# Attention scores of four heads on four 32-row groups of TensorE, strips written through device memory, and GpSimd splitting rotated queries and keys in batches 1 to 7

## What is computed

```python
xn = _layernorm(x, axis=-1)
# attention, on xn
q = (xn @ wq).reshape(B, T, H, D)
lat = xn @ w_down
k = (lat @ wk_up).reshape(B, T, H, D)
v = (lat @ wv_up).reshape(B, T, H, D)
q, k = _apply_rope(q, cos, sin), _apply_rope(k, cos, sin)
scores = einsum('bqhd,bkhd->bhqk', q, k) * scale
allowed = pages[None, :] <= pages[:, None]      # pages of 32 tokens
attn = softmax(where(allowed, scores, min))
s = einsum('bhqk,bkhd->bqhd', attn, v).reshape(B, T, E) @ wo
# experts, on xn: router of two layers, softmax over the best two
y = xn + sum over experts of w * (silu(xn @ ew1 + eb1) @ ew2 + eb2)
out = x + s * silu(y)
```

## Time and profile before

| | us |
|---|---|
| median of 3 runs | 585.58 |
| lowest and highest | 583.09, 585.88 |
| profiled execution | 584.54 |
| its span, first to last instruction | 582.7 |
| mean granted clock of TensorE | 0.938 of full speed |

### The profile page before, as it was taken

One profiled execution on the slowest core, in us unless ns is written; L12 is line 12 of the kernel. 1 busy time (PEld: TensorE's weight loads), 2 busy tenths in 40 slices (PEclk: granted clock), 3 DMA queues, 4 the chain that ended last, 5 costly groups with the idle time before them and its releaser, 6 DMA issues.

```text
span 582.7 us, 9046 instructions
## 1 busy us (share of the span) xinstructions
PE 499.0 (86%) x3223; PEld 327.8 (56%) x3223; DVE 387.7 (67%) x704; ACT 333.9 (57%) x504; POOL 136.7 (23%) x143
## 2 busy tenths in 40 slices
PE   3489997997699878999999999999999987778891
PEld 1256654554356444686776866767767554345450
DVE  4888585897577756836556675557674777568871
ACT  2065573654365435577876767767768543335870
POOL 3120000007664764000000000000001466553620
PEclk9767997999999997999999999999999987789997
DMA  6842216112222322748367263474222225523443
GB/s 176 282 96 102 74 37 165 29 29 82 79 75 61 92 74 65 212 128 238 112 166 190 50 183 100 104 197 118 72 66 59 67 63 161 144 64 101 117 114 90
DMA packets 64676, 64.60 MB, mean 111 GB/s; under 512 B 11096, under 2 KB 48088, under 8 KB 64120
## 3 DMA queue, kind: packets, MB, share of 16 engines
q1 hardware_dynamic: 53616, 47.89, 30.3%
q0 software_dynamic: 4096, 8.40, 5.3%
q10 hardware_dynamic: 6920, 7.74, 4.3%
HBM read 32.27 MB, written 21.24 MB: 92 GB/s over the span
## 4 chain that ended last, share of the span: by engine, by line
PE 65%; DVE 12%; ACT 7%; issue 5%; another core or an unknown queue 4%; DMA 4%; SPq 2%; POOL 1%; ACTq 0%; DVEq 0%; POOLq 0%
PE ring L610 13%; PE wide L650 10%; PE ring L630 9%; PE ring L705 6%; DVE row_max L946 6%; PE ring L695 5%; PE ring L569 4%; ACT probs L807 3%; PE ring L633 3%; PE ring L618 2%; PE ring L662 2%; PE ring L634 2%; PE ring L686 2%; PE ring L560 1%
## 5 line engine op out<-in xcount | busy, mean ns | idle before, releaser
L807 ACT ACTIVATE probs<-ring 128x768 f32<-128x768 f32 (+1 forms) x192 | 164.6, 880 | 147.1 <-PE ring L634 65.9
L946 DVE TENSOR_REDUCE row_max<-ring 128x4 f32<-128x512 f32 (+2 forms) x192 | 195.4, 1042 | 79.3 <-PE ring L610 46.2
L610 PE MATMUL ring<-k_head,q_stack 108*128 108x256 f32 (+2 forms) x512 | 132.8, 373 | 27.1 <-issue 10.9
L1142 POOL DMA_INDIRECT pair_in<-y_rows,place x64 | 62.5, 976 | 265.8 <-PE wide L650 245.2
L610 PEld LDWEIGHTS ring<-k_head,q_stack 108*128 108x128 f32 x512 | 80.6, 203 | 63.6 <-issue 30.1
L1129 POOL DMA_INDIRECT slot_rows<-xn,place x64 | 62.8, 981 | 133.5 <-PE wide L650 109.2
L650 PE MATMUL wide<-probs,v_cols 128*32 128x512 f32 (+3 forms) x1024 | 93.2, 461 | 0.8 <-ACT probs L807 0.8
L630 PE MATMUL ring<-q_stack,k_head 128*128 128x512 f32 (+1 forms) x256 | 82.7, 422 | 13.0 <-ACT probs L807 5.3
L630 PEld LDWEIGHTS ring<-q_stack,k_head 128*128 128x128 f32 x256 | 43.7, 203 | 34.2 <-issue 16.0
L650 PEld LDWEIGHTS wide<-probs,v_cols 128*32 128x32 f32 x1024 | 24.2, 111 | 36.4 <-issue 27.6
L798 ACT ACTIVATE k_head<-k_stack,hmask 128x512 fp32r<-128x512 f32 x64 | 40.8, 712 | 6.5 <-DMA k_stack<-roped_lo 5.4
(11 more groups left out here) (123 smaller groups left out, 500.1 us busy)
## 6 DMA issues: line engine op xcount, KB each, us to landing
area<-w_pack SPq DMA_DIRECT2D x39, 321.0 KB, 3.1
area<-slot_rows SPq DMA_DIRECT2D x39, 128.0 KB, 3.4
y_rows<-work SPq DMA_DIRECT2D x39, 128.0 KB, 2.7
slot_rows<-pair_in ACTq DMA_DIRECT2D x4, 1024.0 KB, 6.0
k_stack<-roped_hi SPq DMA_DIRECT2D x64, 64.0 KB
q_stack<-roped_hi SPq DMA_DIRECT2D x64, 64.0 KB
k_stack<-roped_lo SPq DMA_DIRECT2D x32, 64.0 KB
q_stack<-roped_lo SPq DMA_DIRECT2D x32, 64.0 KB
```

The lines of the kernel that those rows point to most:

```text
L610: last = mm(ps[:, at // T, at % T:at % T + width], q_stack[0:MAX0, g, i * P:(i + 1) * P], k_head[0:MAX0, GH * g + r, 0:width], start=True, ...
L807: activation(probs[:, n % 2, 2 * half:2 * half + 2, lo:T], ps[:, :, lo:T], ACT.Exp, scale=SCALE).then_inc(exp_done, 1)
L946: reduce(row_max[:, g, i, heads[0]:heads[-1] + 1], ps[:, :, 0:(i + 1) * P], AX, ALU.max).then_inc(max_done, 1)
L1142: G.indirect_dma_start(pair_in[:, b % 2, which, t * E:(t + 1) * E], None, y_rows, bass.IndirectOffsetOnAxis(ap=place[:, which, at:at + 1], ...
```

## The change

Every head gets a strip of 32 partitions: 24 rows of data (high, high, low of its 8 columns), 6 rows of mask and 2 of negated maximum. `k_head` and the masking go. A matmul of the maximum or score pass then uses 30 or 32 rows; two neighbours lie on different 32-row groups and write to different banks. Six mask rows are not enough for four tiles of pages, so the second half of the queries is kept twice with other masks (`WIDE` = 768 columns), and the maximum pass always streams 256 keys at a time: six jobs of four matmuls, the first two with the query tiles 0 and 1 for two heads each.

`write` sends the split halves to images in device memory (9 transfers per batch), `read` brings a group's strips back with two transfers. The strips exist twice, by batch parity. Mask rows and ones go into the images once, by 11 constant transfers after the first loads; VectorE rounds them first (`const_ready`). The negated maxima are laid out 128 wide, six matmuls turn them, and VectorE adds the 768 columns from the ring into the query strip; ScalarE's copy and the small transfer go. The copy out of the accumulator moves from VectorE to ScalarE. The split of batch 0 stays on VectorE, those of batches 1 to 7 go to GpSimd; the planner may now look 16 steps ahead on GpSimd too. The next batch's rotation waits for the split of the one before. The last four x are fetched into a part of the expert area. The planner's costs change with it.

```diff
-MAXIMA = ((0, (0, 1, 2, 3)), (1, (0, 1, 2, 3)), (2, (0, 1)), (2, (2, 3)), (3, (0, 1)), (3, (2, 3)))
+MAXIMA = tuple((tiles, first) for tiles in ((0, 1), (2,), (3,)) for first in (0, 2))
...
+STRIP = P // GH
+DATA, MASKED, WIDE = 3 * D, STRIP - 2, T + 2 * P
...
-AT = dict(proj=(-0.59, -0.39, 0.57, 1.45, 1.65, 2.45), router=(0.15, 0.12), heads=-1.58, max=-1.71, max_step=0.1, neg=-1.38, pv=0.64,
+AT = dict(proj=(-0.59, -0.39, 0.57, 1.45, 1.65, 2.45), router=(0.15, 0.12), read=-2.2, max=-1.71, max_step=0.1, neg=-1.38, pv=0.64,
...
+O_COPY = "act"
+SPLIT = ("dve",) + ("pool",) * (B - 1)
...
+            engine = SPLIT[b]
+            add(first[3 + which], engine, ("split", b, which), 2.8 if engine == "pool" else 1.85, (("dve", ("proj", b, which)), 0.1),
+                *([((engine, ("split", b, 0)), 0)] if which else []),
+                *([(("sp", ("write", b - 1, which)), 2.5)] if b else []))
+            add(first[3 + which], "sp", ("write", b, which), (3.9, 1.95)[which], ((engine, ("split", b, which)), 0.1),
+                *([(("sp", ("read", b - 1, NG - 1)), 2.5)] if b else []))
...
-            engine = "dve" if g in DVE_GROUPS else "act"
-            add(first[5] + (g if b else 0.01 * g), "sp", ("stack", b, g), 3.8, (("dve", ("split", b, 1)), 0.1), *used)
-            add(at + AT["heads"] if b or g > 1 else -1.8 + 0.02 * g, engine, ("heads", b, g), 1.9 if engine == "dve" else 2.6,
-                (("sp", ("stack", b, g)), 2.0), *used, *([(("dve", ("consts", 0, 0)), 0.1)] if b == 0 else []))
-            for m, (i, heads) in enumerate(MAXIMA):
-                job(at + AT["max"] + AT["max_step"] * m, ("max", b, NM * g + m), len(heads) * max(2, i + 1) * P / 2200 + 0.06,
-                    "dve", len(heads) * (i + 1) * P / 960 + 0.17, ((engine, ("heads", b, g)), 0.1))
-            add(at + AT["neg"], "dve", ("negate", b, g), 0.37, (("dve", ("max", b, NM * g + NM - 1)), 0.05))
-            job(at + AT["neg"] + 0.01, ("neg_max", b, g), 0.5, "act", 0.59, (("dve", ("negate", b, g)), 0.1))
-            add(at + AT["neg"] + 0.02, "sp", ("neg", b, g), 0.65, (("act", ("neg_max", b, g)), 0.1))
+            at = w0 + g
+            add(first[5] + (AT["read"] + g if b else 0.01 * g), "sp", ("read", b, g), 1.3,
+                *[(("sp", ("write", b, which)), 2.5) for which in range(2)],
+                *([(pv_at(NSTEP * (b - 2) + 3 * g + 2), 0.2)] if b >= 2 else []))
+            for m, (tiles, _) in enumerate(MAXIMA):
+                job(at + AT["max"] + AT["max_step"] * m, ("max", b, NM * g + m), 0.34,
+                    "dve", sum(2 * (i + 1) * P / 960 + 0.1 for i in tiles) + 0.07, (("sp", ("read", b, g)), 2.5))
+            add(at + AT["neg"], "dve", ("negate", b, g), 0.37, (("dve", ("max", b, NM * g + NM - 1)), 0.05), (("dve", ("consts", 0, 0)), 0),
+                *([(("dve", ("neg_max", *divmod(w0 + g - 2, NG))), 0)] if w0 + g >= 2 else []))
+            job(at + AT["neg"] + 0.01, ("neg_max", b, g), 0.7, "dve", 0.87, (("dve", ("negate", b, g)), 0.1))
...
-        for i, step in enumerate(left[e][:LOOK if e != "pool" else 1]):
+        for i, step in enumerate(left[e][:LOOK]):
...
-        q_stack = sb("q_stack", [P, NG, T], F32R)
-        k_stack = sb("k_stack", [P, NG, T])
-        k_head = sb("k_head", [P, H, T], F32R)
+        q_strip = sb("q_strip", [P, 2, NG, WIDE], F32R)
+        k_strip = sb("k_strip", [P, 2, NG, T], F32R)
         row_max = sb("row_max", [P, NG, TT, GH])
-        neg_max = sb("neg_max", [P, NG, TT, MAX_SLOT])
+        neg_max = sb("neg_max", [P, 2, TT, P])
...
+            sp.wait_ge(const_ready, 1)
+            for kind in range(2):
+                rows, low, high = (slice(k, k + 3) for k in (DATA + 3 * kind, 3 * kind, 3 * kind + 6))
+                constant(k_image, rows, slice(0, two), low, 0, 0)
+                constant(k_image, rows, slice(two, T), high, 0, two)
+                constant(q_image, rows, slice(0, T), low, 1, 0)
+                constant(q_image, rows, slice(T, WIDE), high, 1, two)
+            constant(k_image, slice(MASKED, STRIP), slice(0, T), ones_at, 0, 0)
+            constant(q_image, slice(MASKED, STRIP), slice(0, T), zeros_at, 0, 0)
+            constant(q_image, slice(MASKED, STRIP), slice(T, WIDE), zeros_at, 0, 0)
+
+            def write(b, which):
+
+                sp.wait_ge(hi_ready, 2 * b + which + 1)
                 if b >= 1:
...
+                    for g in range(NG):
+                        sp.wait_ge(strips_in[(b - 1) % 2][g], 32 * ((b - 1) // 2) + 32)
+                hi, lo = roped_hi[:, which, :].bitcast(F32), roped_lo[:, which, :].bitcast(F32)
+                for slot, rows in ((0, hi), (1, hi), (2, lo)) if which else ((0, hi), (2, hi), (1, lo)):
+                    if rows is lo:
+                        sp.wait_ge(lo_ready, 2 * b + which + 1)
+                    at = slice(D * slot, D * slot + D)
+                    if which:
+                        sp.dma_start(k_image[:, at, :], rows).then_inc(k_written, 16)
+                    else:
+                        sp.dma_start(q_image[:, at, 0:T], rows).then_inc(q_written, 16)
+                        sp.dma_start(q_image[:, at, T:WIDE], rows[:, 2 * P:T]).then_inc(q_written, 16)
+
+            def read(b, g):
+
+                if b == g == 0:
+                    sp.wait_ge(image_ready, 16 * NCONST)
+                if b >= 2:
+                    sp.wait_ge(pv_done, NSTEP * (b - 2) + 3 * g + 3)
+                sp.wait_ge(q_written, 96 * b + 96)
+                sp.dma_start(q_strip[:, b % 2, g, :].bitcast(F32),
+                             q_image[GH * g:GH * g + GH].rearrange("h x t -> (h x) t")).then_inc(strips_in[b % 2][g], 16)
+                sp.wait_ge(k_written, 48 * b + 48)
+                sp.dma_start(k_strip[:, b % 2, g, :].bitcast(F32),
+                             k_image[GH * g:GH * g + GH].rearrange("h x t -> (h x) t")).then_inc(strips_in[b % 2][g], 16)
...
-                g, (i, heads) = m // NM, MAXIMA[m % NM]
+                g, (tiles, first) = m // NM, MAXIMA[m % NM]
                 if m % NM == 0:
-                    pe.wait_ge(q_in[g], 48 * b + 48)
-                    pe.wait_ge(heads_ready[g], GH * b + GH)
+                    pe.wait_ge(strips_in[b % 2][g], 32 * (b // 2) + 32)
                 ps = take(pe, ("max", b, m))
-                width = max(2, i + 1) * P
-                for k, r in enumerate(heads):
-                    at = k * 2 * T // len(heads)
-                    last = mm(ps[:, at // T, at % T:at % T + width], q_stack[0:MAX0, g, i * P:(i + 1) * P],
-                              k_head[0:MAX0, GH * g + r, 0:width], start=True, stop=True)
+                for part in range(2):
+                    i, keys = tiles[part % len(tiles)], slice(0, 2 * P) if tiles[0] == 0 or part == 0 else slice(2 * P, T)
+                    queries = i * P if keys.start == 0 else T + (i - 2) * P
+                    for r in range(2):
+                        rows = slice(STRIP * (first + r), STRIP * (first + r) + MASKED)
+                        last = mm(ps[:, r, 2 * P * part:2 * P * part + 2 * P], q_strip[rows, b % 2, g, queries:queries + P],
+                                  k_strip[rows, b % 2, g, keys], start=True, stop=True)
                 last.then_inc(slot_full, 1)
 
             def neg_max_t(b, g):
                 pe.wait_ge(neg_ready, NG * b + g + 1)
-                ps = take(pe, ("neg_max", b, g))
-                for i in range(TT):
-                    last = turned(ps[0:MAX_SLOT, 0, i * P:(i + 1) * P], neg_max[:, g, i, :], ident[:])
+                ps = take(pe, ("neg_max", b, g)).rearrange("p a t -> p (a t)")
+                for k, i in enumerate((0, 1, 2, 3, 2, 3)):
+                    last = turned(ps[:, k * P:(k + 1) * P], neg_max[:, g % 2, i, :], ident[:])
                 last.then_inc(slot_full, 1)
 
             def scores(b, e):
                 n, half = divmod(e, 2)
                 g, j = divmod(n, 3)
                 if j == 0 and half == 0:
-                    pe.wait_ge(neg_in[g], 16 * b + 16)
+                    pe.wait_ge(neg_rows_ready, NG * b + g + 1)
                 ps = take(pe, ("scores", b, e))
-                for r in range(2):
-                    h = GH * g + 2 * half + r
-                    if j < 2:
-                        last = mm(ps[:, r, j * P:T], k_head[:, h, j * P:(j + 1) * P], q_stack[:, g, j * P:T],
-                                  start=True, stop=True)
-                    else:
-                        mm(ps[:, r, 0:2 * P], k_head[:, h, 3 * P:T], q_stack[:, g, 2 * P:T], start=True, stop=True)
-                        last = mm(ps[:, r, 2 * P:T], k_head[:, h, 2 * P:3 * P], q_stack[:, g, 2 * P:T],
-                                  start=True, stop=True)
+                keys = (j,) if j < 2 else (3, 2)
+                for k, tile in enumerate(keys):
+                    for r in range(2):
+                        rows = slice(STRIP * (2 * half + r), STRIP * (2 * half + r) + STRIP)
```

(39 more changed lines are left out.)

137 lines of the change are left out of this document (49 added, 88 removed).

## The result

The changed kernel takes **661.5 us** (median of 4, 657.5 to 666.9) where the kernel before takes 585.7 (583.1 to 587.8): a ratio of **1.130, 95% interval 1.119 to 1.141**. The prediction was 549, its range 525 to 588: wrong in sign and far outside the range.

The account below looks back on a forecast made before the run. TensorE alone was taken to bound the dense stretch, TensorE and VectorE together the rest. From 584.54: dense -17, other groups -26, stacking -4, head +6, clock +4, together -37: 547.5, one more for the median: 549 us, range 525 to 588.

Parts of the forecast that it names:

- TensorE's term: Maximum and score matmuls overlap in pairs, -2.46; negated maxima +0.22, shape changes +0.70: net -1.54 us per group.
- B: Rival: in maximum and score jobs, the second pair's weights can't load while the first streams; 598 us, 8%.
- C: Rival: maximum and score matmuls on different row groups don't overlap; +1.15 us per group, 627 us, 6%.
- E: Rival: changes of tile shape on TensorE cost nothing; -22 us, 527 us, 9%.
- VectorE's term: Longer maxima and the added query add, less output copy, masking and most splits: net -1.06 us per group on VectorE.
- So I cost it at nothing: Splits on GpSimd, about 2.8 us each, delay nothing: projections come 1.7 groups (some 20 us) ahead of the first maximum.
- D: Rival: splits behind chunks on GpSimd bring strips late, seven batches wait about 4 us each; +28, 577 us, 12%.
- Head +6: Before the first maximum, SyncE issues 11 constants and 9 writes ahead of the first read: +6 us, bounds +2 and +11.
- Dense stretch, -17: From 237.5 to 441.2 us, experts mixed into attention, TensorE alone bounds: 11 groups x -1.54 = -17 us.
- The other 20 groups, where both engines limit: the mean, so -26: Outside the dense stretch each group gains the mean of TensorE's -1.54 and VectorE's -1.06, -1.3 us: -26 us.
- Clock +4: Outside the dense stretch lighter TensorE work lets its clock fall to 1.2 GHz more often: +4 us, bounds 0 and +14.
- The -4 for the stacking stall: A second set of strips removes half of the 7.9 us wait for the stacking at 85.26: -4 us, bounds 0 and -8.

Follow-up runs that it names:

- e1: Changed kernel with all splits on VectorE: 578.3 us, kernel before 547.3 beside it.
- e2: Changed kernel, splits still on GpSimd but planned ahead of the scatter and gather chunks due after a batch's projections: 586.6 us, ratio 1.072 to the kernel before.
- g4: Kernel before with the splits of batches 1 to 7 on GpSimd, which may pick among 16 steps: 574.0 us, ratio 1.048 to the kernel before.
- k2: Changed kernel with all splits on VectorE and the experts' tables filled later, constants still on SyncE's queue: 615.5 us, ratio 1.050 to the kernel before.
- g3: Changed kernel with all splits on VectorE, constants issued by GpSimd, experts' tables filled after group 1's first maxima: 553.6 us, ratio 1.015 to the kernel before.
- h2: Kernel before with value product of key tiles 1 and 2 cut to 128 query columns, 21 us less TensorE work: 580.8 us, ratio 0.988 to the kernel before.
- k1: Kernel before with each row maximum taken over half of its keys: 583.5 us, ratio 0.978 to the kernel before.
- i3: g3 with each row maximum taken over half of its keys: 543.3 us, g3 561.6 and kernel before 548.1 in the same session.
- i2: g3 with value product of key tiles 1 and 2 cut to 128 query columns: 570.5 us, ratio 1.040 to the kernel before (g3 beside it 1.014).

## Why the prediction was wrong

1. **Overlap, TensorE's term: right.** Starts within 0.02 us, work 56 us less for 48 predicted (31 x 1.54), and 25.5 us for 27 of streaming in the dense stretch, measured. Rivals B (loads block) and C (no overlap) are excluded; E (shape changes free) was not tested by itself. The prediction prices E at 31 x 0.70 = 22 us, but its own sum takes only half of a term outside the dense stretch: 0.70 x 11 and half of 0.70 x 20 are 15. The Trainium skill (TensorE: Matmul & The Clock Gate, Part 3) says that a load overlaps matmuls in flight only on another row group; the trace shows that overlap for the strips (loads of 346.41 and 346.42), and also loads hidden on the same rows, of the full array and of the same strips (151.39), so the rule bounded nothing here.
2. **VectorE's term: right** in size, -31 for -34 us.
3. **"So I cost it at nothing", GpSimd: wrong.** I had the right rival (D) and mis-sized it. The cover, a second projection 1.7 groups ahead, assumed at most one chunk of three between projection and split; the plan has five there, by the places that both were given, and this could be read from the plan before any run. It happens at three batches and not seven, with splits over 20 us late: 22 to 30 us in all (e1, e2, g4), with what the clock adds.
4. **Head +6: mis-sized.** Measured +19 to the first maximum and +24 to the first output copy. I took 0.6 us per issue with an upper bound of 1.07 from the earlier trace rows; the constants took 1.4 and the writes 1.8. The constants are dear in themselves, 1.2 us each in k2 with the tables out of the way, and what is issued beside them is slow too; the tables' filling comes on top (9 to 10 us of the first maximum, against 6 to 7 for the constants). The row of 1.29 already stood above my bound, and no row was of a transfer like these.
5. **Dense stretch, -17 at TensorE's price: mis-sized.** g3 gained 5.7, some 9 when the 23 expert matmuls more in its window are allowed for (312 for 289, 37.8 us busy for 34.7). TensorE's busy time fell by 11, or 14 with the same allowance; the rest is idle time. TensorE's waits for VectorE and ScalarE there rose from 0.7 to 9.9 us (view of the waits, from 240 to 425): it had been busy 98%, but with two partners not far behind it.
6. **"The other 20 groups, where both engines limit: the mean, so -26": this step failed most.** The light stretches of g3 gained nothing, 134.6 for 130.1 and 100.2 for 99.5, +5 with the clock in it. The mean was a guess with no row behind it. h2 gives TensorE's time a worth of a third, k1 and i3 give VectorE's one of a tenth to a fifth. By these, a change of -50 and -34 us brings 17 + 5 = 22 us, not 43.
7. **Clock +4, bounds 0 and +14: wrong by size.** From before to g3 it is 0.96 to 0.88, some 32 us by the estimate above; from before to the changed kernel 0.96 to 0.835, though there part of it follows from the holes of 3 and 4. I had put a tenth more of the light stretches at the lower level; in the changed kernel's second stretch (0.66) it is two thirds.

The parts are, where before takes 547: +61 = 30 (splits) + 25 (head, with the later tables) + 6 (the rest). The first two share 55; how it divides hangs on e1, whose executions lie from 564 to 586. The rest of +6 stands where the sum without head and with splits on VectorE (0.79 us per group back, half of it counted in 20 groups) says about -35. The clock, some 32 where 4 were booked, would explain 28 of the 41, and points 5 and 6 more than the remainder, so these are not independent terms. What separates clock from ring slots stays open: I found no edit that moves one without the other. Also open is what about the lighter work lowers the clock (in i2 it was fewer columns alone), and what makes before take 547 or 588. The -4 for the stacking stall wasn't tested by itself.

## What to carry to other kernels

Price a saving by a cut, not by a share: an engine that is busy 85% may be worth a third of its time, and two engines that pass work through few slots are worth much less than their mean. A step that is moved to another in-order queue costs what the scheduler may put ahead of it, not its own duration: work out the longest such run for every batch, from the plan if there is one. Price an issue by a row of the same kind of transfer. When work is taken from TensorE outside a stretch that it fills, the granted clock may fall; book that as a term of the size of the saving. One cut of 21 us cost g3 14 us and still won the kernel before 7.

## What was not expected of the hardware

- With a fixed order of work, 21 us less matmul made the kernel 14 us slower, the granted clock falling from 0.87 to 0.80 (0.89 to 0.69 in the early stretch).
- Even in the dense stretch the clock fell right behind gaps of TensorE, here in the kernel after. Windows:

```profile
411.00:416.00 5.00, 4.83 (x50) 2.73 (x50) 3.63 (x8) 3.80 (x5) 0.00 (x0) 1.00 0.66 193
416.00:419.00 3.00, 1.99 (x26) 0.83 (x22) 3.00 (x5) 1.62 (x2) 0.00 (x0) 0.99 0.68 182
419.00:423.00 4.00, 4.00 (x23) 3.01 (x21) 2.27 (x4) 1.70 (x2) 0.00 (x0) 0.50 0.73 218
```

  At 2.4 GHz TensorE is busy 4.83 of 5 us; then 1.99 of 3 while VectorE is full; then it is at 1.2 GHz and does 23 matmuls in 4 us, where it had done 50, partly of other shapes, in 5.
- SyncE's issue of the same write took 0.6 us in g3, with the DMA engines at a share of 0.92, and up to 2.5 in the kernel after, behind the constants and at a share of 0.63 (14 to 47). The constants' issues took 1.2 us at 0.29.
- GpSimd needs 1.28 us for adding or subtracting 512 elements on 128 partitions and 0.61 for the conversion, against VectorE's 0.69 and 0.43.
